# Issuing the last two quarters of the first batch's x later in a single-core adapter, mixture-of-experts and shared FFN kernel

## What is computed

```
h   = einsum('bsi,boi->bso', x, weight[adapter_ids])    # one of 8 adapters, 1024x1024, per batch
out = x + moe(h) + shared(h)                            # gated FFNs: top 2 of 16 experts, one shared
```

## Time and profile before

| what | value |
|---|---|
| time, median of 3 runs | 1063.52 us (1063.51 to 1063.78) |
| time of the profiled execution | 1062.65 us |
| its span, first to last instruction | 1060.7 us |
| TensorE, mean granted clock | 0.999 |
| busy: PE, DVE, ACT, POOL | 99%, 60%, 43%, 26% of the span |
| mean DMA rate over the span | 234 GB/s |

### The profile page before, as it was taken

The page is one execution under the profiler, slowest core; times in us unless marked ns, Lnnn a source line. Parts: engine busy times, 40 slices in busy tenths (PEclk is TensorE's granted clock), DMA queues, the critical chain, the costliest instruction groups (busy, mean ns, idle before and its releaser), DMA issues.

```text
span 1060.7 us, 15852 instructions
## 1 busy us (share of the span) xinstructions
PE 1053.1 (99%) x4817; PEld 870.3 (82%) x4818; DVE 634.6 (60%) x652; ACT 457.7 (43%) x529; POOL 275.6 (26%) x325
## 2 busy tenths in 40 slices
PE   8999999999999999999999999999999999999998
PEld 7888888888888888888888888888888888888887
DVE  5766765636756667876766867353553446544454
ACT  6565644532223556665655755332223222322310
POOL 1000000000036655555555650130003200032040
PEclk9999999999999999999999999999999999999999
DMA  8999877422256779986987865763656336464355
GB/s 330 348 365 350 298 282 266 180 80 80 92 211 208 281 269 343 341 331 241 377 346 261 291 242 205 257 219 119 154 224 238 138 119 188 189 238 146 111 192 204
DMA packets 55782, 248.03 MB, mean 234 GB/s; under 512 B 8194, under 2 KB 21634, under 8 KB 45954
## 3 DMA queue, kind: packets, MB, share of 16 engines
q1 hardware_dynamic: 29826, 161.50, 42.5%
q0 software_dynamic: 19008, 62.41, 16.9%
q10 hardware_dynamic: 6912, 23.66, 5.7%
HBM read 200.87 MB, written 43.52 MB: 230 GB/s over the span
## 4 chain that ended last, share of the span: by engine, by line
PE 99%; DMA 1%; SPq 0%; DVE 0%; issue 0%; ACT 0%
PE bank L588 32%; PE bank L590 32%; PE bank L589 32%; PE bank L613 1%; PE bank L826 1%; DMA raw<-cond_w 1%; PE bank L601 0%; PE bank L759 0%; PE bank L622 0%; DMA ids<-ids 0%; SPq L350 0%; PE bank L746 0%; PE bank L794 0%; DVE w_split_sb L1225 0%; DVE rows L1490 0%
## 5 line engine op out<-in xcount | busy, mean ns | idle before, releaser
L1225 DVE TENSOR_TENSOR w_split_sb<-raw,w_split_sb 128x2048 fp32r<-128x2048 f32 (+3 forms) x154 | 257.5, 1703 | 59.7 <-ACT w_split_sb L912 59.2
L912 ACT ACTIVATE w_split_sb<-raw 128x2048 fp32r<-128x2048 f32 (+3 forms) x154 | 216.0, 1439 | 64.2 <-PE bank L590 53.5
L527 POOL DMA_INDIRECT h_in<-h_dram,idx_h x156 | 176.2, 1130 | 124.0 <-DVE tile_f L1539 80.3
L588 PE MATMUL bank<-hT_hi,w_split_sb 128*128 128x512 f32 x512 | 199.8, 390 | 0.0
L589 PE MATMUL bank<-hT_lo,w_split_sb 128*128 128x512 f32 x512 | 199.3, 389 | 0.0
L590 PE MATMUL bank<-hT_hi,w_split_sb 128*128 128x512 f32 x512 | 199.3, 389 | 0.0
L588 PE MATMUL bank<-w_split_sb,tile_hT 128*128 (+1 forms) x312 | 124.8, 400 | 0.0
L590 PE MATMUL bank<-w_split_sb,tile_hT 128*128 (+1 forms) x312 | 122.0, 391 | 0.0
L589 PE MATMUL bank<-w_split_sb,tile_hT 128*128 (+1 forms) x312 | 121.8, 390 | 0.0
L590 PEld LDWEIGHTS bank<-hT_hi,w_split_sb 128*128 128x128 f32 x512 | 96.2, 188 | 20.0
L589 PEld LDWEIGHTS bank<-hT_lo,w_split_sb 128*128 128x128 f32 x512 | 96.2, 188 | 19.8
(11 more groups left out here) (153 smaller groups left out, 1417.6 us busy)
## 6 DMA issues: line engine op xcount, KB each, us to landing
raw<-sh_gu_w SPq DMA_DIRECT2D x16, 2048.0 KB, 9.1
raw<-exp_gu_w SPq DMA_DIRECT2D x16, 2048.0 KB
raw<-cond_w SPq DMA_DIRECT2D x13, 2048.0 KB, 10.1
y_dram<-y_out ACTq DMA_DIRECT2D x39, 512.0 KB, 4.0
raw<-sh_down_w SPq DMA_DIRECT2D x8, 2048.0 KB, 7.7
raw<-exp_down_w SPq DMA_DIRECT2D x16, 1024.0 KB, 8.4
h_dram<-h_blk POOLq DMA_DIRECT2D x16, 512.0 KB, 9.1
x_raw_sb<-xT SPq DMA_DIRECT2D x7, 1024.0 KB, 9.5
```

What stands on the lines that cost most here:

```text
L527: nc.gpsimd.indirect_dma_start(out=h_in[par][:, i, :], out_offset=None, in_=h_blocks, in_offset=bass.IndirectOffsetOnAxis(ap=idx_h[par][:, ...
L588: nc.tensor.matmul(dst, lhs[0], rhs[0], start=first, stop=False)
L912: return nc.scalar.activation(dst, src, ACT.Copy)
L1225: return nc.vector.tensor_tensor(dst, src, hi.bitcast(F32), ALU.subtract)
```

## The change

The issue of x2 moves from behind the copy of x0 to behind the copy of w0, and the issue of x3 moves from behind the copy of w0 to behind the copy of w2. Nothing else differs: same transfers, same copies in the same order, same waits.

```
                 copy(x_split_sb[0][:, 0, k0:k1, :]..., x_raw_sb[:, k0 * SEQ:k1 * SEQ]).then_inc(first_hi, 1)
-                if i == 0:
-                    first_x_load(2)
                 for k in (2 * i, 2 * i + 1):
                     act.wait_ge(first_w[k], 16)
                     copy(w_split_sb[:, 0, 0, k * HALF:(k + 1) * HALF], raw[0][:, k * HALF:(k + 1) * HALF]).then_inc(first_hi, 1)
-                    if k == 0:
-                        first_x_load(3)
+                    if k in (0, 2):
+                        first_x_load(2 + k // 2)
```

## The result

The changed kernel took 1066.92 us in the median of 11 runs (1065.18 to 1069.70), the kernel before 1062.96 us in 11 runs of the same measurement (1062.52 to 1063.78). The ratio is 1.0037, 95% interval 1.0026 to 1.0047: 2.8 to 5.0 us slower. The profiled execution took 1067.65 us with a span of 1065.8, against 1062.65 and 1060.7. The eleven runs scatter over 4.5 us where before they scattered over 1.3, and they fall into two groups by the mean granted clock that each run reports: five at 1.000 took 1065.18 to 1066.47 (median 1065.62), six at 0.996 to 0.998 took 1066.92 to 1069.70 (median 1068.26).

The account below looks back on a forecast made before the run. PE was taken as the bound from 12.26 us to its last matmul. Early gains vanish inside the new wait before k = 6, +1.8 and +0.1 make +1.9 us: 1065.4 us on the median of 1063.52, range 1063.5 to 1068.1.

Parts of the forecast that it names:

- the forecast's own case: x3 lands behind s1, so PE waits before k = 6: +1.9 us, 1065.4 us; chance 0.38.
- B: Rival, slower by more: x3 behind s2 or s3 (1066.7 or 1068.1), or the clock falls (1066.8); chance 0.36.
- The shared line: ACT's and SP's queues form one line: an ACT transfer starts when those already issued by SP are through.
- D: Rival, small gain: ACT's transfers have their own turns beside SP's; -1.2 to +0.2 us, at best 1062.3; chance 0.13.
- Step (1): Issue times on ACT: x2 goes out at 6.41, x3 when w2 lands; no added instructions, cost 0.
- Step (2): Before k = 2: w2 without x2 in front lands at 9.5, PE starts 1.2 us earlier (bounds 0.6 to 1.4).
- Step (3): Before k = 4: x2 lands at 12.7 or up to 0.64 sooner; PE 0.3 to 0.9 us ahead, no harm.
- Step (4): Before k = 6: x3, issued at 9.5, lands when s1 did; +1.8 us, and +0.1 for the slow first k.
- The clock: At PE's new wait: clock may fall to 1.2 GHz, costing 1.4 us, or 0 if it holds; chance 0.10.
- Step (5): Behind k = 6: PE does not wait again and the later load of the next x is covered; 0 us.

Follow-up runs that it names:

- hold_s: The changed kernel, with SP waiting for the end of the copy of w2 before issuing s0 to s3: 1063.18 us, ratio 1.0001 to the kernel before.
- x3_only: Against the kernel before, only x3's issue moved, from behind the copy of w0 to behind that of w2: 1064.84 us, ratio 1.0018.
- sp_order: Against the kernel before, x2 and x3 issued by SP, in front of w4 and w6, not by ACT: 1062.15 us, ratio 0.9993.
- after_fill: The changed kernel with 45 matmuls on the tile of ones put in front of PE's wait before k = 4: 1065.73 us, ratio 1.0026 to before.
- x2_only: Against the kernel before, only x2's issue moved, to behind the copy of w0, where x3 already was: 1067.56 us, ratio 1.0041.
- pool_late: The changed kernel with x2 and x3 issued by POOL on its own queue, behind the copies of w0 and w2: 1067.91 us, ratio 1.0047 to before.

## Why the prediction was right, and where it was not

The direction held, and the mechanism in outline: a transfer issued from ACT is held up by what SP has already issued, the s pieces make the wait (hold_s takes all of it away), PE carries it undiminished to the end. The measured median lies inside the range. It is not the forecast's own case: +1.9 us was forecast, +4.0 was measured. That is near the number of B, "slower by more" (1066.7 for an x3 behind s2, 1066.8 for a fallen clock), but B's first condition did not come: the wait is x2's, before k = 4, and no case of the prediction has it. In the profile 3.65 us of it and 1.45 us of clock make nearly all of the loss; in the five runs whose clock held, the loss is 2.7 us. That the median lies in the range is in part luck.

*The shared line.* Held for the first part of the wait only. x2 and x3 took 8.7 and 9.3 us to landing in the changed kernel, against 6.2 and 6.3, but x2 stood in a line for 3.5 us of it; for the other 5.2 us it shared the engines with the s pieces. "Starts when those already issued by SP are through" was read from the gate load, whose window ended too soon. The next 2.8 us of the kernel before, from 17.4 to 20.2, in which s2 and s3 came in:

```profile
q1 hardware_dynamic: 193, 1.11, 96.5%
q10 hardware_dynamic: 139, 0.06, 8.0%
```

There the gate load's packets already went in between SP's. Strict order fell in the runs too: in x3_only x3 landed before s1 and s2. D, whose turns were to bring an x piece in after 3.7 to 6.3 us, fell as well, even for POOL's queue. The Trainium skill (DMA: Bandwidth & Descriptors, Queues, rings and completion order) says that each DMA engine goes round-robin, packet by packet, between the queue rows for which it has work. The trace agrees with this from 11.5 us on (275 packets of q10 beside 385 of q1; how many of them make one turn isn't shown). By itself the rule doesn't give the 3.5 us before, in which q10 had none.

*Step (1).* Held for the code, and hid the failure. x2 goes out with the copy of w0 (x3 even 0.4 us ahead of the copy of w2, at 9.38 against 9.78, as ACT was still in the copy of x1); but the step put w0's landing at the 6.4 us of the one profile before. In the twelve profiles of this study the copy of w0 starts below 7 us in three (the kernel before, sp_order, after_fill) and at 7.4 to 8.2 in nine, kernels with x2 in its old place among them. An issue that hangs on a landing inherits its scatter.

*Step (2).* Failed in its size. w2 was no longer waited for, but PE was not ahead: k = 0 started 1.63 us later. At 14.83 + 0.23 = 15.06 PE could have begun k = 4, before it was at 15.10. The gain of 1.2 us was nil in this profile. x2 is also not the whole cause that I took it for: sp_order has the wait before k = 2 without x2 there. As a part of the cause it is borne out by the twelve profiles, though no run isolates it: w2 took 5.7 to 6.8 us with x2 beside it, and 3.7 to 5.2 in seven of the eight profiles without.

*Step (3)* is the step that failed: "It lands where x3 did, 12.7", so that nothing is lost at k = 4. x2 met s0, which SP, not slowed by an x piece in its line, issued at 7.51 (8.65 before), and landed at 16.75, 4 us later than the step had it. With w0 early (after_fill) the step comes close: 13.1. The chain behind it, 2.12 us from landing to PE, is confirmed: 16.75 to 18.87.

*Step (4)* gave the right number in x3_only (+1.8 measured, +1.8 and 0.1 forecast for this wait), but not for its reason: x3 was issued at 10.09, behind s2, where the line in order of issue would have brought it in at 18.8 or later (the prediction's own B), and it landed 1 us before s1. In after_fill x3 was issued at 8.11, behind s0 and s1 alone, and landed at 18.2, 10.1 us later, where the step had 17.5. In the changed kernel x3's wait is hidden behind x2's.

*The clock.* It stood among B's chances with 0.10; it fell in 6 of 11 runs and again in 5 of 6. Its price was forecast as 0 to 1.4 us: k = 4 and 5 took 1.45 us longer. The price rested on a low stretch of 2.8 us at the start of the launch (the granted clock reads 1.00 in both of those rows; only the pace of the matmuls told the levels apart); the measured one was 3.4 us. The two groups of runs lie 2.6 us apart, which is more than this price. One reason is at hand: in the profiles of x2_only and pool_late the low stretch lasted 6.8 us, and the lowest mean clocks, 0.996 and 0.997, belong there. Whether the runs with a low clock also had the longer waits isn't shown, as only one run of each kernel has a trace.

*Step (5)*, no cost behind k = 6, held: the starts of k = 6 differ by 5.22 us, the spans by 5.1.

## What to carry to other kernels

A DMA issue placed behind a compute instruction that waits for a landing is issued at the moment of that landing. Here it then waited 2.6 to 4.0 us for its first packet, whatever its queue, and had to share the engines with the bulk after that; count what the other queues have issued by then, not the distance in the code. Urgent transfers belong in the issue order of the queue that carries the bulk, ahead of it (sp_order), or the bulk must be held back (hold_s); a queue of their own, ACT's or POOL's, did not spare them the wait. Before trusting a date from one profile, look at the same date in several: here the landing of the first weights moved by 1.8 us between profiles and with it changed the product that waited.

## What the runs showed of the hardware that I had not expected

A transfer on POOL's queue needed 8.4 us to landing behind SP's pieces, no less than one on ACT's (8.7). Yet x3 in x3_only, issued 0.6 us after s2, landed 2.3 us before it, and 1 us before s1. The packets say how a late issue can overtake: once the x pieces have packets, these go in between those of the s pieces, about one to one (275 beside 385), and an x piece has half the bytes of an s piece. What makes up the 2.6 to 4.0 us before the first packet stays open.

The clock need not fall inside the wait. In x3_only PE stood from 17.61 to 19.79, and the windows show the fall after it had restarted:

```profile
18.00:19.00 1.00, 0.00 (x0) 1.00 0.85 340
19.00:20.00 1.00, 0.21 (x1) 1.00 0.44 172
20.00:21.00 1.00, 1.00 (x4) 0.73 0.96 211
21.00:22.00 1.00, 1.00 (x4) 0.50 1.02 428
```

So a wait of 2.2 us was followed by a fall in this run; eight of the eleven runs of the same kernel report a mean of 1.000, though how long PE waited in those isn't known. And the low stretch is not always of one length: 3.4 us in the changed kernel (18.3 to 21.7), 6.8 us in x2_only and pool_late.
